# A gated linear attention stage: state update on TensorE, decays through DRAM, moments on ScalarE, projections and the sigmoid in other places

## The reference, cut to what matters

```python
q = feature_map((x @ Wq.T) * SCALE)      # elu + 1, 16 heads of 16
k = feature_map(x @ Wk.T)
v = x @ Wv.T
gate = sigmoid(x @ Wg.T + bg)            # one per token and head
def step(S, inp):
    S = g_t[:, :, None, None] * S + k_t[..., :, None] * v_t[..., None, :]
    y_t = einsum('bhi,bhij->bhj', q_t, S)
x = layernorm(x + y @ Wo.T)              # 4 sequences x 1024 tokens x 256
```

## Time and profile before

| what | before |
|---|---|
| device time, three runs | 1454.76, 1460.06, 1461.71 us (median 1460.06) |
| the profiled execution: its time, its span | 1467.62 us, 1465.6 us |
| attention stage in that span | 0 to about 325.9 us |
| busy share over the whole span | TensorE 92%, VectorE 57%, ScalarE 37%, GpSimd 21% |
| granted TensorE clock over the whole span | 0.979 of full speed |

### The profile page before, as it was taken

How to read it: one execution, slowest core, us unless ns; L and a number is a source line. 1 busy time by engine, 2 the same in 40 slices (tenths; PEclk the granted TensorE clock), 3 DMA queues, 4 the chain that set the end, 5 groups by cost and what they waited for, 6 DMA issues and landing times. The chain is left out here.

```text
span 1465.6 us, 21869 instructions
## 1 busy us (share of the span) xinstructions
PE 1345.6 (92%) x7418; PEld 859.6 (59%) x7419; DVE 828.9 (57%) x1676; ACT 536.7 (37%) x1104; POOL 305.6 (21%) x357
## 2 busy tenths in 40 slices
PE   7888888889989899999999997869999999899996
PEld 4556656655545566666666664436665564477774
DVE  5999999986533222222222221457778755676774
ACT  5445554432011122222222221134444532457675
POOL 2133333321653000000000001613220000144444
PEclk9899999999999999999999999989999999999999
DMA  5544544629221011111111112303110000000001
GB/s 192 177 171 172 177 170 158 207 80 370 84 79 61 22 51 43 43 47 46 43 43 50 43 43 90 87 21 105 30 29 1 1 1 11 1 1 15 29 15 58
DMA packets 68226, 112.39 MB, mean 77 GB/s; under 512 B 9008, under 2 KB 53936, under 8 KB 64048
## 3 DMA queue, kind: packets, MB, share of 16 engines
q1 hardware_dynamic: 61584, 94.49, 19.2%
q0 software_dynamic: 6144, 16.79, 3.6%
q10 hardware_dynamic: 416, 0.03, 0.0%
HBM read 79.70 MB, written 31.59 MB: 76 GB/s over the span
## 5 line engine op out<-in xcount | busy, mean ns | idle before, releaser
L1684 POOL DMA_INDIRECT m_got<-outs,slot x64 | 61.2, 957 | 562.7 <-DMA outs<-XT 448.1
L1089 DVE TENSOR_TENSOR ro_h<-ro_bB,ro_sl 128x512 f32<-128x512 f32 x71 | 49.1, 692 | 218.5 <-PE ro_bB L1038 218.5
L515 DVE TENSOR_TENSOR_SCAN a_dcy<-a_gbc,a_ident 128x2048 f32<-128x2048 f32 x32 | 144.6, 4520 | 11.2 <-DMA a_gbc<-gd 7.3
L2040 POOL TENSOR_TENSOR q_hr<-q_hf,q_hr 128x512 fp32r<-128x512 f32 x64 | 83.9, 1322 | 287.0 <-ACT q_hr L1881 287.0
L1033 PE MATMUL ro_bA<-Win,ro_xT 128*128 x284 | 135.9, 601 | 0.7 <-ACT ro_xT L1060 0.6
L1045 PE MATMUL ro_bO<-Wout,ro_hT 128*128 x568 | 134.3, 379 | 0.9 <-DVE ro_hT L1082 0.9
L1045 PEld LDWEIGHTS ro_bO<-Wout,ro_hT 128*128 128x128 f32 x568 | 107.8, 190 | 45.6 <-issue 34.6
L1038 PE MATMUL ro_bB<-Wsw,ro_xT 128*128 x284 | 133.5, 592 | 0.0
L1082 DVE COPY ro_hT<-ro_bH 128x512 f32<-128x512 f32 x71 | 49.1, 691 | 101.2 <-PE ro_bH L1018 101.2
L1069 ACT ACTIVATE XT<-ro_bO 128x256 f32<-128x256 f32 x71 | 27.2, 383 | 204.9 <-PE ro_bO L1045 204.9
L1038 PEld LDWEIGHTS ro_bB<-Wsw,ro_xT 128*128 128x128 f32 x284 | 54.0, 190 | 68.2 <-issue 68.2
(11 more groups left out here) (271 smaller groups left out, 2524.1 us busy)
## 6 DMA issues: line engine op xcount, KB each, us to landing
a_gbc<-gd SPq DMA_DIRECT2D x32, 1024.0 KB, 4.8
rows<-a_zero SPq DMA_DIRECT2D x8, 1152.0 KB, 10.5
XT<-rows SPq DMA_DIRECT2D x71, 128.0 KB, 2.0
outs<-XT SPq DMA_DIRECT2D x71, 128.0 KB, 1.7
a_xt<-in_xTt SPq DMA_DIRECT2D x8, 512.0 KB, 3.7
X<-in_x SPq DMA_DIRECT2D x8, 512.0 KB, 5.8
Win<-in_w_in SPq DMA_DIRECT2D x8, 512.0 KB, 10.7
Wsw<-in_w_sw SPq DMA_DIRECT2D x8, 512.0 KB, 10.6
```

What stands on the lines that cost most here:

```text
L515: v.tensor_tensor_scan(dcy[:, :], gbc[j % 2][:, :], ident16[:, :], 0.0, ALU.mult, ALU.add).then_inc(d_done, 1)
L1684: pool.indirect_dma_start(out=got[q % 2][k][:, t, :], out_offset=None, in_=mem["outs"], in_offset=bass.IndirectOffsetOnAxis(ap=slot[:, k, ...
L2040: pool.tensor_tensor(hr[:, 1, f % 4, :], hf[f % 2][:, :], hr[:, 0, f % 4, :], ALU.subtract).then_inc(hl_done, 1)
```

## The change

- **State update.** TensorE now adds the decayed state itself: after the eight k-times-v products it multiplies `dg`, a diagonal matrix of 32 x 32 per block with the tile's last decay on it, with `St`, and adds it to the same PSUM columns. ScalarE makes `dg` (two instructions of 128 x 32). VectorE keeps one instruction, mask into `St`.
- **Decays.** The products with `rep`, and `rep` itself (512 KB from DRAM), are gone. `ET` is stored to DRAM (four transfers per chunk), and each tile's decays come back on all partitions, in two transfers into one of four buffers `ebc`. `decayed_q` reads `ebc` in place of PSUM; the copy `dec` is gone. Chunk 0, which has no state before it, gets no scan for `ET`.
- **Moments.** `bn_stats` and `bn_aggr` are gone from VectorE. ScalarE makes the negative mean and the sum of squares, by two activations over 256 columns with an accumulator output, two iterations later. `spread` has one instruction less. Turn, router and normalize of a tile come two iterations later, and the loop has two more iterations at its end.
- **Places.** `project` stands ahead of `attend` on TensorE, and ahead of `y_out` on ScalarE, in three of four steps. On ScalarE `gates` stands behind `project` and `values` of the gate step, where it stood ahead of `y_out`. On VectorE `gate_decay` stands behind the weigh of the next iteration, where it closed the gate step. `phi` of the first four quarters is on VectorE.

```diff
@@ SyncE
+                def decays_out(T):
+                    sp.wait_ge(e_done, T)
+                    for b in range(B):
+                        sp.dma_start(mem["ed"][T, b], ET[T % 2][32 * b:32 * b + H, :]).then_inc(ed_out, 16)
+                def decays_in(j):
...
+                    for g in range(G):
+                        sp.dma_start(ebc[j % 4][:, g, :], mem["ed"][T, b, 8 * g:8 * g + 8, :].unsqueeze(1).to_broadcast([8, DH, P])).then_inc(eb_in[j % 4], 16)
@@ TensorE
-                def decays(j):
...
-                        mm = pe.matmul(bK[:, HALF + g * P:HALF + (g + 1) * P], rep[:, b, g, :], ET[T % 2][:, :], start=True, stop=True)
-                    mm.then_inc(er_ready, 1)
...
+                    if j >= 4:
+                        pe.wait_ge(dg_done, 2 * (j - 3))
+                        pe.wait_ge(st_done, j - 3)
+                        for g in range(G):
+                            for r in range(4):
+                                mm = pe.matmul(bK[32 * r:32 * r + 32, 32 * g:32 * g + 32], dg[j % 2][32 * r:32 * r + 32, g, :],
+                                               St[32 * r:32 * r + 32, j % 4, g, :], start=False, stop=True, skip_group_check=True)
...
+                    if Q < NT and Q % 4 > 0:
+                        project(Q)
@@ ScalarE
+                def decay_matrix(j):
...
+                    for g in range(G):
+                        act.activation(dg[j % 2][:, g, :], eye32[:, :], ACT.Copy, scale=ebc[j % 4][:, g, P - 1:P]).then_inc(dg_done, 1)
...
+                def moments(j):
...
+                    act.activation(scrap[:, :], X[:, j, :], ACT.Copy, scale=-1.0 / D, accum_out=mv[T % 2][:, b, 0:1]).then_inc(bn_done, 1)
+                    act.wait_ge(bn_done, j + 1)
+                    act.activation(scrap[:, :], X[:, j, :], ACT.Square, bias=mv[T % 2][:, b, 0:1], accum_out=mv[T % 2][:, b, 1:2]).then_inc(ag_done, 1)
...
                     if tile(n + 1):
                         values(n + 1)
-                    if carries(n - 6):
-                        keep_x(n - 6)
-                    if carries(n - 5):
-                        normalize(n - 5)
+                    if 0 < Q < NT and Q % 4 == 0:
+                        gates(Q // 4)
+                    if carries(n - 8):
+                        keep_x(n - 8)
+                    if tile(n - 2):
+                        moments(n - 2)
+                    if carries(n - 7):
+                        normalize(n - 7)
@@ VectorE
-                    v.tensor_tensor(um[:, :, :], bK[:, 0:64].rearrange("p (g c) -> p g c", g=G), blk[:, :, :], ALU.mult).then_inc(um_done, 1)
...
-                    for g in range(G):
-                        v.scalar_tensor_tensor(out=St[:, b, g, :], in0=St[:, b, g, :], scalar=dec[j % 2][:, g:g + 1], in1=um[:, g, :],
-                                               op0=ALU.mult, op1=ALU.add).then_inc(st_done, 1)
+                    v.tensor_tensor(St[:, b, :, :], bK[:, 0:64].rearrange("p (g c) -> p g c", g=G), blk[:, :, :], ALU.mult).then_inc(st_done, 1)
...
                     if tile(n):
                         weigh(n)
+                    if n >= 0 and n % 4 == 0 and n // 4 + 1 < NC:
+                        gate_decay(n // 4 + 1)
                     if carries(n - 1):
                         update(n - 1)
```

More of the change, by code:

```diff
@@ L593, in _ @@
                         residual(n - 1)
-                    if Q % 4 == 0 and Q < NT:
-                        gate_decay(Q // 4)
+                    if n == FIRST:
+                        gate_decay(0)
+                    if Q < 4:
+                        phi(Q)
             @block.gpsimd
@@ L2132 @@
     gate_b[:, :H] = a["L0_attn_bg"]
-    spread = np.zeros((B, 32, B, D), np.float32)
-    for b in range(B):
-        spread[b, :H, b] = np.arange(H)[:, None] == head[None, :]
     def columns(v):
@@ L2159 @@
         "ident": np.eye(P, dtype=np.float32),
-        "rep": spread.reshape(P, B, G, P),
         "hmask": ((p[:, None] // 16) % 2 == np.arange(2)[None, :]).astype(np.float32),
+        "eye32": np.tile(np.eye(32, dtype=np.float32), (4, 1)),
         "blk": np.stack([(p[:, None] // 16) % 2 == np.arange(32)[None, :] // 16] * G, axis=1).astype(np.float32),
```

168 lines of the change are left out of this document (77 added, 91 removed).

## The result

| | before | after |
|---|---|---|
| median, us | 1459.63 (20 runs) | 1454.05 (20 runs) |
| lowest to highest, us | 1454.01 to 1463.14 | 1450.09 to 1458.73 |
| profiled execution: span, us | 1465.6 | 1456.9 |
| first, 5th, 29th, 32nd weigh, us | 24.33, 62.28, 291.85, 316.80 | 24.24, 60.29, 288.33, 310.61 |
| end of the attention stage, us | 325.98 | 326.87 |

The ratio is 0.9969, with an interval of 0.9958 to 0.998: 4.5 us less by the ratio (the medians differ by 5.6), where 15.4 were forecast. Neither profiled execution is a typical one: that of before took 1467.62 us, above all its 20 runs, and that of after 1458.73, the highest of its 20. The last row is the surprise.

The account below looks back on a forecast made before the run. VectorE was taken to set the attention step, TensorE about a microsecond behind. Head -3, groups -14.8, last steps -1.8, end +4.2 sum to -15.4 us: 1445 us from median 1460.06, own range 1435 to 1453, full range 1433 to 1460.

Parts of the forecast that it names:

- the ordinary step: Attention stage, weigh to weigh on VectorE: from 9.14 to 8.1 us, with TensorE's chain equal at 8.09.
- TensorE's new products: Eight 32 x 32 products added to TensorE's step: 0.27 us taken, 0.54 as upper bound.
- The head: Stage start up to tile 4's weigh at 62.28: -3 us, from 0 to -5.
- The group: Four steps between tiles 4 and 28: 36.05 us against 38.52, so -14.8 us over six groups.
- 3.1 us of waiting plus 0.55: VectorE waits 3.1 us for the late sigmoid, then pays 0.55 for gate_decay: 3.65 us per group.
- 4 x 8.1: The rest of each group: four steps at 8.1 us each, besides the 3.65 us of stall and gate_decay.
- the wait for x: TensorE's gates wait for the chunk's x, whose landing takes 3.7 us: 0.4 us per group.
- the gates' broadcast: Transfer of 4.8 us behind four more issues on SyncE, landing within half a microsecond of the scan reading it.
- The end: Tiles 28 to 31: three steps save 1.8 us; two more iterations and ScalarE's last passes add 4.2.
- A: Rival: the sigmoid is hidden and the 3.1 us per group vanish, about -21 us, 1424 us; chance 0.12.
- B: Rival: TensorE's clock falls after each stall, 2.55 us lost seven times, +17.9, 1463 us; chance 0.18.
- C: Rival: gates reach the scan late, 2 us in each of six groups, 1457 us; chance 0.12.

Follow-up runs that it names:

- stats_vector: early_sp with bn_stats and bn_aggr back on VectorE behind the residual and no moments on ScalarE; ratio 0.991 to before, 1460.03 us.
- the new order on SyncE: Next tile's broadcasts (gates, decays) issued ahead of the stores of gates and decays on SyncE; alone on the changed kernel, ratio 0.9958 to before.
- sigmoid_early: Changed kernel with the sigmoid again ahead of y_out on ScalarE, gate_decay still behind weigh; ratio 0.9781 to before, 1443.44 us.
- the dummy products: Changed kernel with six unused TensorE products added between scores and project_out in each gate iteration; ratio 0.9973 to before.
- gd_behind_kw: Changed kernel with VectorE's gate_decay moved behind weigh_k and ahead of the scan; ratio 0.9973 to before.
- early_sp: Changed kernel with the sigmoid ahead of y_out and SyncE's broadcasts ahead of the stores, gate_decay unmoved; ratio 0.9792 to before, 1442.42 us.
- early_sp_tail: early_sp with normalize ahead of the moments on ScalarE; ratio 0.9774 to before, 1440.23 us.
- combo: Changed kernel with the sigmoid ahead of y_out, gate_decay behind the scan, and broadcasts ahead of the stores on SyncE; ratio 0.988 to before.

## Why the prediction was wrong, point by point

**What bounds the kernel, and the ordinary step: right.** 7.94 us instead of the 8.1 forecast, and by stats_vector 0.70 of the 1.20 us gained come from the statistics. TensorE's new products take 0.26 us from start to start, as assumed (0.27).

**The head: right in size, half by luck.** From 62.28 to 60.29 is -2.0, where -3 was forecast; against the other three profiles of before (65.4 to 65.5) it is -5.1 to -5.4. That the profile of before was one of the rarer early starts I couldn't see in it, but a row of 5.12 us for a scan that takes 4.42 elsewhere stood in it and said that two engines met there.

**The group: here the forecast failed.** The term "3.1 us of waiting plus 0.55" was 3.54 + 0.54 in the step shown, and 3.2 to 3.5 us of waiting in four of the six groups (1.76 in the first, 7.94 in the bad one), so the stall itself was well sized. From the start of the table load to that of the sigmoid pass 180.75 - 179.46 = 1.29 us. The Trainium skill, page "ScalarE: Activation LUTs", section "What ACT_TABLE_LOAD costs", has 2.66 us with a drain for it; the trace contradicts that again. The failing step is the term 4 x 8.1 for the rest of the group. Behind the waiting `gate_decay` I named mask, weigh_k and scan, but not who waits for weigh_k: TensorE's `project_out`. So TensorE stood too, 2.1 to 2.4 us in each of the six groups, lost its clock, and was late by 1.4 us in the next step: 11.78 + 9.41 + 7.94 + 8.35 = 37.48 us in the group from 250.85, where the forecast had 36.05 (11.75 + 3 x 8.1). The fourth step, 8.35 instead of 8.1, holds TensorE's gate products. Over the six groups the new kernel takes 288.33 - 60.29 = 228.04 us, 11.7 more than 6 x 36.05: 6.2 of it in the group with the step of 16.51 us, 1.3 to 2.0 in each of four others, and 0.6 less than forecast in the first. And before takes 291.85 - 62.28 = 229.57, not 6 x 38.52 = 231.1, since its first and last groups are 0.8 and 0.5 us shorter than the one I measured. The gain is 1.5 us instead of 14.8.

**The transfers: underrated.** I took the wait for x as 0.4 us per group and the gates' broadcast as just in time. The broadcast hardly cost anything here (one wait of 0.91 us). The transfer of x did: 0.5 to 0.9 us in four groups and 2.36 in one, where TensorE's half clock behind it made a step of 16.51 us. Why x landed late there is not shown; it did so in both profiles of the changed kernel, and also in two runs with the new order on SyncE.

**The end: mis-sized.** +7.1 us (16.3 - 9.2) where +4.2 was forecast. I priced two more iterations at the old 1.42 us and the passes of two tiles at 1.4, but normalize stands behind the moments on ScalarE, and turn_x waits for normalize: a ring of 2.43 to 2.68 us. Against the 10.7 to 10.8 us of the other three profiles of before it is +5.5 to +5.6. Only the last three steps helped, 22.28 us instead of 24.95, -2.7 where -1.8 was forecast.

**The rivals.** A, the sigmoid hidden, was priced at 21 us against the forecast; sigmoid_early makes it true, and the stage is 19.9 us shorter. B, the falling clock, was the mechanism that took about half of the gain per group, 1.3 of 2.47 us. Its price was too high, since the slow stretch was on the path for 1.3 us (9.41 less 8.11 with the dummy products) and not for 2.55. It got 0.18; the argument against it, that the rest would be split by the update's products, overlooked the longer rest that came from weigh_k. C, late gates, did not happen in the changed kernel and did in gd_behind_kw.

The sum by measured terms, against the profile that I used: head -2.0, groups -1.5, last steps -2.7, end +7.1, together +0.9 us, as the stage ends show (326.87 - 325.98). Against the other three profiles of before it is about -5.2 for the head, -1.8 for the groups, -2.7 for the last steps and +5.5 to +6.9 for the end, some -3 to -4 us, which fits the ratio. That 1454 lies between 1433 and 1460 says little for the forecast: it is above the forecast's own range of 1435 to 1453, in the part that was added for the rivals. That the first pair of profiles lay 8.7 us apart in span came from later stages, which the change does not touch. For the kernel before they took 1126.2 to 1140.2 us from one chip to another, and on one chip 1138.4 us in early_sp and 1146.9 in early_sp_tail, which are the same there; so a few us of the stage can't be seen in the time of one profile.

## What to carry to other kernels

When a wait is put in front of a step, list what is queued behind it on that engine, then for each of these who waits for it on other engines, and follow it until someone has slack; an engine that was 1 us from being the bound has none. A late producer is better cured by moving the producer forward or by placing its consumer in time that is idle anyway; doing two such moves at once added nothing here and was slower than the better one alone (0.988 against 0.978). And a row that is longer than its like in one place of the trace (5.12 us instead of 4.42) is a meeting of two engines whose outcome may differ in the next execution.

## What the runs showed of the hardware

TensorE's clock fell after rests that I had thought harmless, and the length of the rest alone did not decide. In the changed kernel it fell after 2.1 to 2.4 us in one piece in all six groups, at once (Wo 1.86 instead of 1.13 us, Wqk 2.86 instead of 1.88) or a product later (at 102.78, after 2.38 us, Wo took 1.10 and Wqk 3.25; the granted clock was 1.00 from 102.7 to 103.9 and 0.53 from 103.9 to 107). In the kernel before, the same rest went either way: after 2.32 us ahead of one tile's scores Wo took 1.03 in one profile, and after 2.33 us 1.75 to 1.91 in the other three. So did two short rests close together: 0.66 and 1.30 us in combo were followed by a granted clock of 0.50 (180 to 182), 0.67 and 1.30 in another group of that run, and 0.89 and 1.30 in early_sp, by scores of 1.15 us. After 1.18 us alone it did not fall. What decides between them no run here shows.

Reading an accumulator on ScalarE is an instruction of its own of 0.18 to 0.22 us; the moments of a tile keep the engine for 1.04 us from the first start to the next instruction's (320.28 to 321.32), against the two passes' 0.41 and 0.51. A start 0.06 us behind VectorE's scan cost GpSimd 4.1 us. One transfer of x was in use 3.8 to 5.6 us after its issue, from one run to another, at the same place of the program.
